# Routing chunk 0's first token tile ahead of its other three

## What is computed

```python
x = layernorm(x + block1(x))      # rmsnorm, 3-tap conv and scan along the sequence, then a 512-wide gated MLP
scores = sigmoid(x @ gate_w.T)    # 64 experts in 8 groups of 8
choice = scores + gate_bias
# of each token: a group's worth is the sum of its two best; 4 groups stay; of those the 8 best experts
rw     = scores of the 8, divided by their sum, times 2.5
routed = sum over the 8 of rw * (silu(x @ Wg[e].T) * (x @ Wu[e].T)) @ Wd[e].T
shared = (silu(x @ Sg.T) * (x @ Su.T)) @ Sd.T
out    = layernorm(x + routed + shared)
```

## Time and profile before

| | us |
|---|---|
| median of three runs (lowest, highest) | 660.44 (659.85, 661.64) |
| the profiled execution | 660.38 |
| its span, from the first to the last instruction | 658.5 |
| PE, DVE, ACT, POOL busy | 590.1, 460.9, 323.9, 448.2 |
| first scatter on POOL | 56.38 |
| first and last gather on POOL | 355.10, 649.4 |

### The profile page before, as it was taken

One profiled execution on the slowest core, in us unless ns is written; L12 is line 12 of the kernel. 1 busy time (PEld: TensorE's weight loads), 2 busy tenths in 40 slices (PEclk: granted clock), 3 DMA queues, 4 the chain that ended last, 5 costly groups with the idle time before them and its releaser, 6 DMA issues.

```text
span 658.5 us, 13356 instructions
## 1 busy us (share of the span) xinstructions
PE 590.1 (90%) x3456; PEld 472.7 (72%) x3457; DVE 460.9 (70%) x1311; ACT 323.9 (49%) x633; POOL 448.2 (68%) x464
## 2 busy tenths in 40 slices
PE   3976988888888999999997999999999999999980
PEld 2645656654555899999994999999995666666640
DVE  3456688878756889776773567677475598868785
ACT  8564876655553455455541445555552135253332
POOL 1004777777777777777776777777764777777773
PEclk9997999988997999999997899999999999999995
DMA  8962667651112687877754688888876123222122
GB/s 240 353 134 56 148 151 157 139 132 53 52 52 90 177 236 233 240 221 226 222 163 133 175 234 236 238 227 235 224 202 208 52 54 93 57 67 67 52 64 64
DMA packets 124605, 101.32 MB, mean 154 GB/s; under 512 B 15334, under 2 KB 114494, under 8 KB 124094
## 3 DMA queue, kind: packets, MB, share of 16 engines
q1 hardware_dynamic: 63766, 48.41, 27.6%
q0 software_dynamic: 14336, 29.39, 15.5%
q10 hardware_dynamic: 46464, 23.07, 12.2%
HBM read 52.58 MB, written 48.23 MB: 153 GB/s over the span
## 4 chain that ended last, share of the span: by engine, by line
PE 76%; DVE 9%; ACT 6%; issue 4%; POOL 3%; DMA 1%; POOLq 0%; DVEq 0%; ACTq 0%
PE GU L814 16%; PE OT L834 12%; PE XT L803 6%; PE HT L823 6%; PE OT L616 4%; PE GU L874 4%; PE GU L875 4%; PE XT L883 4%; PE GU L595 3%; PE GU L596 3%; POOL arena L512 3%; PE GU L745 2%; PE GU L746 2%; ACT x1r L962 2%; DMA arena<-os_dram,gslots 1%
## 5 line engine op out<-in xcount | busy, mean ns | idle before, releaser
L507 POOL DMA_INDIRECT xs_dram<-x1r,slots x224 | 227.6, 1016 | 121.8 <-issue 67.8
L512 POOL DMA_INDIRECT arena<-os_dram,gslots x224 | 218.4, 975 | 79.5 <-issue 66.7
L814 PE MATMUL GU<-wgu_sb,arena 128*128 x704 | 121.3, 316 | 0.1
L814 PEld LDWEIGHTS GU<-wgu_sb,arena 128*128 128x128 f32 x704 | 106.4, 192 | 0.8 <-issue 0.5
L834 PE MATMUL OT<-wd_sb,arena 88*128 x704 | 95.2, 278 | 1.7 <-ACT ol L1088 1.7
L1492 DVE TENSOR_TENSOR mlpw_sb<-GU,mlpw_sb 128x352 f32<-128x352 f32 x88 | 46.1, 524 | 67.8 <-ACT mlpw_sb L1078 61.2
L1088 ACT ACTIVATE ol<-OT 128x512 f32<-128x512 f32 x88 | 52.6, 597 | 83.1 <-PE OT L834 82.2
L834 PEld LDWEIGHTS OT<-wd_sb,arena 88*128 88x128 f32 x704 | 86.3, 193 | 3.6 <-issue 2.6
L1554 DVE SCALAR_TENSOR_TENSOR x_all<-arena,wk,x_all 128x128 f32<-128x128 f32 x224 | 66.3, 345 | 4.7 <-DMA arena<-os_dram,gslots 2.9
L1078 ACT ACTIVATE mlpw_sb<-GU 128x352 f32<-128x352 f32 x88 | 40.9, 464 | 48.7 <-PE GU L814 44.5
L1167 ACT ACTIVATE key<-GU 128x512 f32<-128x512 f32 x44 | 26.3, 597 | 69.9 <-PE GU L875 69.9
(11 more groups left out here) (205 smaller groups left out, 898.2 us busy)
## 6 DMA issues: line engine op xcount, KB each, us to landing
arena<-xs_dram SPq DMA_DIRECT2D x352, 64.0 KB
os_dram<-ol ACTq DMA_DIRECT2D x88, 256.0 KB
xs_dram<-ol SPq DMA_DIRECT2D x16, 512.0 KB, 4.4
wgu_sb<-wgu_dram SPq DMA_DIRECT2D x1, 5632.0 KB
xs_dram<-x1r,slots POOLq DMA_INDIRECT x224
arena<-os_dram,gslots POOLq DMA_INDIRECT x224
wd_sb<-wd_dram SPq DMA_DIRECT2D x1, 2816.0 KB
x_all<-x_dram SPq DMA_DIRECT2D x8, 256.0 KB, 5.7
```

Source lines behind the costliest of these rows:

```text
L507: g.indirect_dma_start(out=xs[b], out_offset=bass.IndirectOffsetOnAxis(ap=slots[:, t * K + k:t * K + k + 1], axis=0), in_=x1r[:, t, :], in ...
L512: return g.indirect_dma_start(out=gbuf[:, g_ % 2, t - SETS[g_][0], k, :], out_offset=None, in_=os[batch_of(t)], in_offset=bass.IndirectOff ...
L814: ins = mm(GU[:, 2 * r + i // 2, (i % 2) * 2 * I:(i % 2 + 1) * 2 * I], xg[:, r, i * P:(i + 1) * P], wgu_sb[:, bass.ds(at[i], 2 * I)], star ...
```

## The change

DVE's five routing functions get a range of tiles (`first`, `end`); for chunk 0 they run once for tile 0 alone and once for tiles 1 to 3. PE gets `first_ranks`, two matmuls for tile 0, and DVE `take_first_ranks`. POOL waits for tile 0's slots at tile 0, and for `s_slot` of chunk 0 at tile 1. The diff, cut to its core:

```diff
@@ gpsimd, before the 8 scatters of tile t @@
                 if t % CT == 0:
                     pool.wait_ge(s_x1r, t // CT + 1)
+                if t == 0:
+                    pool.wait_ge(s_slot_e, 1)
+                elif t == 1:
+                    pool.wait_ge(s_slot, 1)
+                elif t % CT == 0:
                     pool.wait_ge(s_slot, t // CT + 1)
@@ tensor @@
             def ranks(c):
+                first = 1 if c == EARLY else 0
                 pe.wait_ge(s_sel, c + 1)
-                if c:
+                if c == EARLY:
+                    pe.wait_ge(s_key_e, 1)
+                else:
                     pe.wait_ge(s_key, c)
-                mm(HT[:, 0:CT * E], ones_bf[:, :], base_bf[:, :].unsqueeze(1).to_broadcast([P, CT, E]),
+                mm(HT[:, first * E:CT * E], ones_bf[:, :], base_bf[:, :].unsqueeze(1).to_broadcast([P, CT - first, E]),
...
+            def first_ranks():
+                pe.wait_ge(s_sel_e, 1)
+                mm(HT[:, 0:E], ones_bf[:, :], base_bf[:, :], start=True, stop=False, skip_group_check=True)
+                mm(HT[:, 0:E], upto_bf[:, :], sel[:, 0, :], start=False, stop=True,
+                   skip_group_check=True).then_inc(p_rank_e, 1)
@@ step(k) @@
                 if mlp:
                     mlp_block(k - 1, 1)
+                if c == EARLY:
+                    first_ranks()
@@ vector @@
-            def group_sums(c):
+            def group_sums(c, first=0, end=CT):
...
+            def take_first_ranks():
+                dve.wait_ge(p_rank_e, 1)
+                v.tensor_tensor(key[:, 0, :], HT[:, 0:E], sel[:, 0, :], ALU.mult).then_inc(s_key_e, 1)
+                dve.wait_ge(s_key_e, 1)
+                then(v.max(keys[:, 0, :], key[:, 0, :]))
+                v.tensor_scalar(slots[:, 0:K], keys[:, 0, :], float(P - 1), None, ALU.add).then_inc(s_slot_e, 1)
@@ vector, the loop over k @@
                 if c == EARLY:
-                    group_sums(c)
+                    group_sums(c, 0, 1)
+                    group_seconds(0, 1)
+                    compare_groups(0, 1)
+                    mask_groups(0, 1)
+                    choose(c, 0, 1)
                 if mlp:
                     hidden(k - 1, 0)
                     hidden(k - 1, 1)
                 if c == EARLY:
-                    group_seconds()
-                    compare_groups()
-                    mask_groups()
-                    choose(c)
+                    take_first_ranks()
+                    group_sums(c, 1, CT)
+                    group_seconds(1, CT)
+                    compare_groups(1, CT)
+                    mask_groups(1, CT)
+                    choose(c, 1, CT)
                     hidden(k - 1, 2)
                     hidden(k - 1, 3)
                     take_ranks(c)
```

More of the change, by code:

```diff
@@ L311, in build @@
         s_sel = sem("s_sel")
+        s_sel_e = sem("s_sel_e")
         p_rank = sem("p_rank")
+        p_rank_e = sem("p_rank_e")
         s_key = sem("s_key")
+        s_key_e = sem("s_key_e")
         s_nt = sem("s_nt")
@@ L316, in build @@
         s_slot = sem("s_slot")
+        s_slot_e = sem("s_slot_e")
         s_gslot = sem("s_gslot")
@@ L656, in ranks @@
                            skip_group_check=True)
-                ins = mm(HT[:, 0:CT * E], upto_bf[:, :], flat(sel[:, ring(c), :]), start=False, stop=True,
-                         skip_group_check=True)
+                ins = mm(HT[:, first * E:CT * E], upto_bf[:, :], flat(sel[:, ring(c), :])[:, first * E:], start=False,
+                         stop=True, skip_group_check=True)
                 if c in CLAST:
@@ L1289, in _ @@
             ch4, ta4, tb4 = (a.rearrange(by_group, e=EG) for a in (choice, tab_a, tab_b))
-            def group_sums(c):
+            def group_sums(c, first=0, end=CT):
                 dve.wait_ge(s_sc, c + 1)
[L1295 to L1311, removed]
+                n = slice(first * NG, end * NG)
@@ new lines, in group_sums @@
+                then(v.tensor_tensor(choice[:, first:end, :], score[:, first:end, :],
+                                     bc(gbias_sb[:, :].unsqueeze(1), P, end - first, E), ALU.add))
+                lo, hi = ch4[:, n, 0:EG // 2], ch4[:, n, EG // 2:EG]
+                v.tensor_tensor(ta4[:, n, 0:4], lo, hi, ALU.max)
+                then(v.tensor_tensor(ta4[:, n, 4:8], lo, hi, ALU.min))
+                v.tensor_tensor(tb4[:, n, 0:2], ta4[:, n, 0:2], ta4[:, n, 2:4], ALU.max)
+                v.tensor_tensor(tb4[:, n, 2:4], ta4[:, n, 0:2], ta4[:, n, 2:4], ALU.min)
@@ new lines, in group_sums, with group_seconds @@
+                then(v.tensor_tensor(tb4[:, n, 4:6], ta4[:, n, 4:6], ta4[:, n, 6:8], ALU.max))
+            def group_seconds(first=0, end=CT):
+                n = slice(first * NG, end * NG)
+                then(v.tensor_tensor(tb4[:, n, 6:8], tb4[:, n, 2:4], tb4[:, n, 4:6], ALU.max))
+                v.tensor_tensor(pairs[:, n, 0:1], tb4[:, n, 0:1], tb4[:, n, 1:2], ALU.add)
+                then(v.tensor_tensor(pairs[:, n, 1:3], tb4[:, n, 0:2], tb4[:, n, 6:8], ALU.add))
+                then(v.tensor_reduce(gs[:, n], pairs[:, n, :], AX_X, ALU.max))
@@ L1312, in compare_groups @@
+            def compare_groups(first=0, end=CT):
+                for i in range(first, end):
                     ins = v.max(gtop[:, i, :], gs[:, i * NG:(i + 1) * NG])
                 then(ins)
-                then(v.memset(gtop[:, :, TOPG:NG], NOWHERE))
-                for i in range(CT):
+                then(v.memset(gtop[:, first:end, TOPG:NG], NOWHERE))
+                for i in range(first, end):
                     ins = v.match_replace(out=m1[:, i * NG:(i + 1) * NG], in_to_replace=gtop[:, i, :],
@@ L1318, in compare_groups, with mask_groups, choose @@
                 then(ins)
[L1320 to L1329, removed]
+            def mask_groups(first=0, end=CT):
+                n, own = (end - first) * NG, slice(first * NG, end * NG)
+                then(v.tensor_scalar(m2[:, own], m1[:, own], GONE, None, ALU.is_equal))
+                then(v.tensor_tensor(ch4[:, own, :], ch4[:, own, :], bc(m2[:, own].unsqueeze(2), P, n, EG), ALU.mult))
+                then(v.tensor_scalar(choice[:, first:end, :], choice[:, first:end, :], 0.0, None, ALU.add))
+            def choose(c, first=0, end=CT):
+                for i in range(first, end):
                     ins = v.max(top[:, i, :], choice[:, i, :])
                 then(ins)
-                for i in range(CT):
+                for i in range(first, end):
                     ins = v.match_replace(out=tab_a[:, i, :], in_to_replace=top[:, i, :], in_values=choice[:, i, :],
@@ L1335, in choose @@
                 then(ins)
+                own = slice(c % 4 * CT + first, c % 4 * CT + end)
+                done_sel = s_sel_e if (c, first) == (EARLY, 0) else s_sel
                 if c >= 4:
                     dve.wait_ge(p_rank, c)
-                then(v.tensor_scalar(sel[:, ring(c), :], tab_a, GONE, None, ALU.is_equal))
-                v.tensor_tensor(rw[:, span(c), :], sel[:, ring(c), :], score, ALU.mult).then_inc(s_sel, 1)
+                then(v.tensor_scalar(sel[:, own, :], tab_a[:, first:end, :], GONE, None, ALU.is_equal))
+                v.tensor_tensor(rw[:, c * CT + first:c * CT + end, :], sel[:, own, :], score[:, first:end, :], ALU.mult).then_inc(done_sel, 1)
             def take_ranks(c):
+                first = 1 if c == EARLY else 0
+                own = slice(c * CT + first, (c + 1) * CT)
                 dve.wait_ge(p_rank, c + 1)
-                v.tensor_tensor(flat(key[:, span(c), :]), HT[:, 0:CT * E], flat(sel[:, ring(c), :]),
+                v.tensor_tensor(flat(key[:, own, :]), HT[:, first * E:CT * E], flat(sel[:, ring(c), :])[:, first * E:],
                                 ALU.mult).then_inc(s_key, 1)
                 dve.wait_ge(s_key, c + 1)
-                for t in tiles(c):
+                for t in tiles(c)[first:]:
                     ins = v.max(keys[:, t, :], key[:, t, :])
                 then(ins)
-                v.tensor_scalar(slots[:, c * CT * K:(c + 1) * CT * K], flat(keys[:, span(c), :]), float(P - 1), None,
-                                ALU.add).then_inc(s_slot, 1)
+                v.tensor_scalar(slots[:, (c * CT + first) * K:(c + 1) * CT * K], flat(keys[:, own, :]), float(P - 1),
+                                None, ALU.add).then_inc(s_slot, 1)
+            def take_first_ranks():
[4 more added lines that the diff above has]
+                v.tensor_scalar(slots[:, 0:K], keys[:, 0, :], float(P - 1), None, ALU.add).then_inc(s_slot_e, 1)
             def count_tiles(b):
```

## The result

Seven runs of the changed kernel have a median of 664.92 us (663.61 to 665.90); seven of the kernel before, taken with them, 661.53 (659.85 to 664.57). The ratio is 1.0046 (95% interval 1.0026 to 1.0065), some 3.0 us slower, 1.7 to 4.3. The profiled execution took 665.5 us with a span of 663.6, 5.1 more than the span before.

What follows compares the result with a forecast made beforehand. It took PE's chain of waits as the bound, with DVE's time up to chunk 0's `conv` on the path. DVE's split (+2.7) and PE's clock (+0.7) summed to +3.4 on 660.44, giving 663.8 us, range 661.0 to 665.7.

Steps and rivals of the forecast that it cites:

- The lead is given back at scatter 32: On POOL: the first scatter comes 5.7 us earlier, but scatter 32 waits for chunk 1's slots and comes 3.4 later.
- DVE's time up to conv is on the path: In chunk 0's step: DVE's time up to the last `conv` product counts microsecond for microsecond up to the end.
- The price of the split: On DVE before `conv`: more instructions and broken series cost 3.8 us, less 1.04 of old waits, +2.7 us.
- PE's clock: On PE at blocks 2 and 3: idling brings a half-rate spell, taking 1.6 us from PE, +0.7 on the path.
- Everything behind moves alike: After `conv`: squares, chunk 1's slots, scatters, both batches' first transposes and the first gather all come later by the same amount.
- a delay at `conv` found again at 214 us: Sign at batch 0's start: if the delay at `conv` is not found again there, the whole prediction is wrong.
- cheap splits (1): Rival on DVE's split: cheap instructions and no cold spell on PE, +1.3 to +2.0, 661.7 to 662.4 us; 15%.
- The lost later cold spell (3): Rival on PE around `spread`: PE keeps its clock, 1.8 us come back, ending at -0.5, 659.9 us; 7%.
- POOL as the bound (4): Rival: POOL's nearly unbroken list bounds the kernel, and the lead of 5.7 carried through gives 654.7 us; 5%.
- A longer cold spell (2): Rival on PE before `ranks`: idling brings about 7 us at half rate, DVE waits 2.6 for the ranks, 665.7 us; 8%.

Runs made afterwards that it cites:

- e1: The changed kernel, but POOL's first scatter again waits for the slots of all four tiles: 664.89 us, 1.0063 of the kernel before.
- e4: The changed kernel with chunk 2's conv products moved ahead of chunk 0's routing on DVE: 655.63 us, 0.9927 of the kernel before.
- e2: The kernel before with DVE's chunk 0 routing run for tile 0, then tiles 1 to 3, in the old order: 663.86 us, ratio 1.0047.
- e5: The kernel before with DVE's chunk 0 routing run three times (tile 0, tile 1, tiles 2 and 3): 666.09 us, ratio 1.0068.
- e3: The kernel before with chunk 2's conv products moved ahead of chunk 0's routing on DVE: 660.24 us, ratio 0.9986.
- e6: e4 with chunk 2's square sums moved ahead of the last two mlp_down on PE: 655.05 us, 0.9897 of the kernel before.

## Why the prediction was right

It said 663.8 us, +3.4 over before and slower with 73%; measured were 664.92, and +3.0 (1.7 to 4.3) as the ratio. The lower end of its range should be 661.1 by its own terms, not 661.0; nothing hangs on that.

- *The lead is given back at scatter 32.* Right, and shown twice: the gap grew to 10.05 (some 9 said), and e1, without the lead, is as slow. The first scatter came at 52.05 (50.7 said) and the squares at 63.24 (61 to 62 said); 1.63 of both lies ahead of the scores. e4 shows from the other side that the lead has a value once chunk 1's slots are early enough.
- *DVE's time up to conv is on the path.* Right: e2 and e5 add nothing but DVE instructions there and delay the squares and scatter 32; e3 takes conv out of it and the front gains.
- *The price of the split.* Said 3.8, less 1.04; measured 3.44, less 1.04. The narrowest instructions were overrated: 16 and 32 wide took 0.17 to 0.19 us, not 0.22 like the 64-wide, so tile 0 cost 4.52 in place of 4.9. The Trainium skill's formula ("VectorE: DVE Perf Modes", section on the TRN2 errata) agrees with single durations: it makes 0.174 us of 16 elements, and the row shows 0.17. The prediction's estimate from it for the split, 2.8, came out low against 3.44. The broken series and the waits between instructions are not in it; that they make the difference was not tested.
- *PE's clock.* Said +0.7 by the nearest row; the wait for the ranks was 0.73 in the changed kernel, 0.90 in e1. In e1 the spell is the one described: it takes 1.64 from PE, and 1.6 was said. In the changed kernel's profiled execution PE was at the low level from before the routing to past 52, for a reason that is not the change's, so that 0.73 comes so close to 0.7 is in part luck.
- *Everything behind moves alike.* Right for chunk 1's slots (4.67 later) and the scatters (4.6), but too simple for PE. At batch 0 PE's branch was 3.0 later, and the loads ended last by 0.60; at batch 1 the first transposes are 4.87 later, with the wait for the shared experts as before (0.79, 0.78), and the first gather 5.18. PE's later falls to the low clock last longer in one execution than in another, 1.6 us in this pair and 1.85 in e1, which is as much as half of the effect. The prediction took that part of the path as fixed; by its own sign, a delay at `conv` found again at 214 us, the trace of e1 taken alone would have spoken against it (3.30 at the squares, 0.53 at 214).

Of the rivals, cheap splits (1), at +1.3 to +2.0, are excluded by the rows (2.40 net on DVE and 0.73 of waiting) and by e5's price, though not by the time alone, whose interval begins at 1.7. The lost later cold spell (3) is excluded by `spread` still at 2.08, POOL as the bound (4) by e1. A longer cold spell (2) in its own sense, from the idle time that the change makes, did not come: in e1 the clock is back before 52. The profiled execution has a spell of some ten microseconds, but it began ahead of the routing, and DVE waited 0.73 for the ranks, not 2.6.

Open: the two parts of the +3.1, DVE's 2.4 and PE's 0.7, were told apart inside the traces only; the measured time would allow the first alone. No kernel was timed that keeps the new order and spares PE the idle time.

## What to carry to other kernels

Before work is brought forward for an engine, find its next appointment: the one gap in a long row of equal ones (0.74 among 0.30) told that POOL's start had no value of its own. Then look what the move lengthens on the engine that keeps that appointment. And before rejecting the idea, look whether the second gate can be opened too: DVE had stood idle for 4 us just ahead of the routing, conv fitted into them, and with it the same change went from 0.5% slower to 0.7% faster.

## What the runs showed of the hardware that was not expected

DVE's fp32 TENSOR_TENSOR instructions on 8 to 64 elements per partition cost nearly the same: 0.16 to 0.19 us at 8 and 16 wide, 0.18 to 0.22 at 32, 0.21 to 0.23 at 64, while 256 take 0.42. So cutting a 256-wide one in 64 and 192 costs 0.23 + 0.35 in place of 0.42. PE's falls to the low clock differ between executions of the same instructions: after the same 2.06 us of idle time the third pair of matmuls took 1.91 us in one and 1.02 in the other. And the stretch of POOL's scatters 32 to 64 takes 42.2 us in e1, e4 and e6, 42.8 in e3, but 43.7 in the kernel before, the changed one, e2 and e5, with the same instructions (some of them take up to 1.96 us in place of 0.96): a spread of 1.5 us whose cause stays open.
